# Attention output projection: VectorE adds each tile to the residual straight from PSUM, in place of a ScalarE copy and a GpSimd sum

## The chip, the core and the metric

The kernel runs on one core of a Trainium2 chip. The metric is the device time of one execution in microseconds (us), the median of several runs. A core has TensorE (PE in the profile: matmuls and transposes; PEld is its weight load), VectorE (DVE), ScalarE (ACT) and GpSimd (POOL), each with its own queue that it works off in order, and SyncE, which starts DMA transfers. Engines wait for each other by semaphores. Matmul results land in PSUM, which has eight banks of 128 partitions by 512 float32 values.

## The reference, cut to what matters

One pre-norm decoder layer on `x` of shape (4, 512, 512): attention, a small cross attention, and a mixture of experts. The change touches the end of the attention:

```python
q = (xn @ Wq.T).reshape(B, L, 32, 64)      # 32 query heads
k = (xn @ Wk.T).reshape(B, L, 8, 64)       # 8 key/value heads
v = (xn @ Wv.T).reshape(B, L, 8, 64)
q, k = rope(q), rope(k)
p = softmax(causal(q @ k.T) / 8)
out = (p @ v).reshape(B, L, 2048)
x = x + out @ Wo.T                         # the change is in this line
```

Every float32 matmul is made of products of a high and a low part (`_hi`, `_lo`): ACT writes the rounded high part, and DVE or POOL subtracts it from the source to get the low part.

## The kernel before, in words

Everything stays in SBUF during the attention: the residual `x_res`, the normalised input `xn_hi`, `xn_lo`, and the weights of one key/value group. The outer loop runs over the 8 groups (`GROUPS`), inside it over the 4 batches (b = 0 to 3), inside that over the 4 query heads of the group (h = 0 to 3). The work of one (b, h) is called a slot here; there are 16 in a group and 128 in all. In a slot the heads are software-pipelined. For slot c = 4b + h, PE issues, in this order:

- the last two transposes of the head two before (`pe_ptrans`, u = 2, line 218), which wait until DVE has made `pt_lo` from the bank that they overwrite;
- the scores of the next head (line 208);
- for h = 0, 1, 2 a projection of the next batch (line 185, 12 matmuls), for h = 3 only four small transposes of v (line 195);
- in slot h = 0 an output projection (t = 2, line 247);
- eight transposes of the previous head (u = 0 and 1, line 218), the first of which wait until DVE has made the `pt_lo` of the u = 2 transposes above;
- probabilities times v (line 235);
- in slots h = 1, 2 and 3 an output projection (t = 3, 0 and 1, line 247).

So there is one output projection of 128 tokens (`pe_wo`, six matmuls into the bank `WO_BANK`) in each slot, 128 in all. Before the change ACT copies the bank to SBUF (`act_wo`, line 372, `wo_out`, two buffers), and POOL adds the copy to the residual (`pool_woacc`, line 562). ACT, DVE and POOL have orders of their own, written out by hand. For DVE in a slot: `dve_masked` (line 434: four rows of the next head's scores plus mask, with a row maximum), `pt_lo` for u = 2, in even slots `o_lo` (line 422), in slots h = 0 and h = 2 the two `q_st` low parts (lines 459 and 460), in slot h = 2 of b = 1 the two low parts of the output weights (`w_lo`, line 422), for h < 3 the rotary multiply and shuffle (lines 452 and 453), a reciprocal (line 441), `pt_lo` for u = 0 and 1, and `dve_oadd` (line 487, `o_f`), which waits for ACT's `act_opart`. For POOL in a slot: for h = 1 `k_lo` (line 554), for h < 3 the rotary sum (lines 537 and 539), the normalisation of the probabilities (`pool_norm`, line 546, four pieces), the sum of the change (line 562), and in slots h = 1, 2, 3 of b = 2 the low part of one third of the next group's projection weights (`w1_lo`, line 469, also called `w_lo` in the rows).

The next output projection waits on `wo_out_done`, since there is one bank. The last group's last batch has no next batch to project, and its four output projections come at the very end, each in a bank of its own. After the attention a second block begins (cross attention and routing), and after it the experts, in which the change touches nothing.

Of the kernel before, what the change touches and what calls it, by code (L numbers as in the profile page):

```python
# [21 lines left out]
ALU = mybir.AluOpType  # L22
ACT = mybir.ActivationFunctionType
# [43 lines left out]
def wait(eng, sem, value):  # L67

    if isinstance(value, int) and value <= 0:
        return  # L70
    eng.wait_ge(sem, value)
# [27 lines left out]
def decoder_layer(nc, x, ctx, ctx_cols, mem_mask, wqkv, wo_rows, router_cols, router_b, gu_w, gu_b, down_w, down_b,  # L99
                  cos_t, sin_t, causal_t, ident_t, iota_t, out):  # L100
    stack = ExitStack()
    with stack:
# [24 lines left out]
        def sa(name, shape, dt=F32):  # L127
            return attn.enter_context(nc.sbuf_tensor(name, shape, dt))
# [14 lines left out]
        v_st = sa("v_st", [P, 2, QB, P], F32R)  # L143
        rot = sa("rot", [P, L])
        rope = sa("rope", [P, 2, L])
        wo_out = sa("wo_out", [P, 2, D])
        v_and_o = sa("v_and_o", [P, L])
        o_part, v_t = v_and_o[0:HD, :], v_and_o[HD:P, :]
        o_f = sa("o_f", [P, L])
# [12 lines left out]
            "w2_lo_done", "proj_done", "vt_done", "rope_in", "rot_sin", "rope_sum", "rope_hi", "k_lo_done", "q_lo_done",  # L162
            "v_tr", "v_hi_done", "v_lo_done", "scores_done", "masked_done", "exp_done",
            "recip_done", "pnorm_done", "ptrans_done", "pt_hi_done", "pt_lo_done", "pv_done", "opart_done",
            "oadd_done", "o_hi_done", "o_lo_done", "wo_done", "wo_out_done", "woacc_done")}

        def settled(eng):

# [196 lines left out]
            wait(act, s["wo_done"], 4 * m - 4)  # L365
            act_split(o_st[0][:, k, :], o_f[:, :], s["o_hi_done"])

        def act_wo(act, m, t, src=WO_BANK):

            act.wait_ge(s["wo_done"], 4 * m + t + 1)  # L370
            wait(act, s["woacc_done"], 4 * m + t - 1)
            nc.scalar.activation(wo_out[:, t % 2, :], src[:, :], ACT.Copy).then_inc(s["wo_out_done"], 1)  # L372

        def act_group(act, g, r):

            for c in range(HEADS + (isinstance(g, int) and g == GROUPS - 1)):
                b, h = divmod(c, G)
                n, m = HEADS * g + c, B * g + b
                front = c < HEADS
                begun = not (isinstance(g, int) and g == 0 and c == 0)  # L380
                more = not (isinstance(g, int) and g == GROUPS - 1 and c >= HEADS - 1)
                next_batch = not (isinstance(g, int) and g == GROUPS - 1 and b >= B - 1)
                d = c - 1
                db, dh = divmod(d, G)
                dn_, dm = HEADS * g + d, B * g + db
                d_here = not (isinstance(g, int) and g == 0 and d < 0)
                d_begun = not (isinstance(g, int) and g == 0 and d < 1)
                d_last = not (isinstance(g, int) and g == 0 and db < 1)
                d_before_last = not (isinstance(g, int) and g == 0 and db < 2)
                if d_begun:  # L390
                    act_pt(act, dn_ - 1, (d + 1) % 2, 2)
                if h == 0 and begun and front:
                    act_rope(act, m, 2, b % 2)
                if h in (1, 2) and next_batch:
                    act_rope(act, m + 1, h - 1, (b + 1) % 2)
                if more:
                    act_exp(act, n + 1, (r + c + 1) % 3)
                if h == 0 and next_batch:
                    act_vt(act, m + 1, 3 * m + 4)
                if d_here:  # L400
                    act_pt(act, dn_, d % 2, 0)
                    act_pt(act, dn_, d % 2, 1)
                if dh == 3 and d_last:
                    act_wo(act, dm - 1, 2)
                if h == 3 and next_batch:
                    act_v(act, m + 1, (b + 1) % 2)
                if d_begun:
                    act_opart(act, dn_ - 1)
                if dh in (1, 2) and d_last:
                    act_wo(act, dm - 1, dh - 1)  # L410
                if dh == 0 and d_before_last:
                    act_wo(act, dm - 2, 3)
                if d_begun and dh % 2 == 0:
                    act_o(act, dn_ - 1, dm if dh else dm - 1, (d // 2 - 1) % 4)
                if dh == 0 and db == 1:
                    act_w2(act, g)
                if (b, h) in W1_SLOTS and not (isinstance(g, int) and g == GROUPS - 1):
                    act_w1(act, g + 1, W1_SLOTS[b, h])
# [70 lines left out]
        def dve_o(dve, pair, k):  # L489
            dve.wait_ge(s["o_hi_done"], pair + 1)  # L490
            dve_lo(o_st[1][:, k, :], o_f[:, :], o_st[0][:, k, :], s["o_lo_done"])

        def dve_group(dve, g, r):

            for c in range(HEADS + (isinstance(g, int) and g == GROUPS - 1)):
                b, h = divmod(c, G)
                n, m = HEADS * g + c, B * g + b
                front = c < HEADS
                begun = not (isinstance(g, int) and g == 0 and c == 0)
                more = not (isinstance(g, int) and g == GROUPS - 1 and c >= HEADS - 1)  # L500
                next_batch = not (isinstance(g, int) and g == GROUPS - 1 and b >= B - 1)
                d = c - 1
                db, dh = divmod(d, G)
                dn_, dm = HEADS * g + d, B * g + db
                d_here = not (isinstance(g, int) and g == 0 and d < 0)
                d_begun = not (isinstance(g, int) and g == 0 and d < 1)
                d_last = not (isinstance(g, int) and g == 0 and db < 1)
                d_before_last = not (isinstance(g, int) and g == 0 and db < 2)
                if more:
                    dve_masked(dve, n + 1, (r + c + 1) % 3)  # L510
                if d_begun:
                    dve_pt(dve, dn_ - 1, (d + 1) % 2, 2)
                if d_begun and dh % 2 == 1 and not (isinstance(g, int) and g == 0 and d == 1):
                    dve_o(dve, HEADS // 2 * g + (d - 1) // 2 - 1, ((d - 1) // 2 - 1) % 4)
                if h == 0 and begun and front:
                    dve_q_lo(dve, m, 2, b % 2)
                if h == 2 and next_batch:
                    dve_q_lo(dve, m + 1, 1, (b + 1) % 2)
                if dh == 1 and db == 1:
                    dve_w2(dve, g)  # L520
                if h < 3 and next_batch:
                    dve_rope_in(dve, m + 1, h, (b + 1) % 2)
                if more:
                    dve_recip(dve, n + 1, (r + c + 1) % 3)
                if d_here:
                    dve_pt(dve, dn_, d % 2, 0)
                    dve_pt(dve, dn_, d % 2, 1)
                if h == 3 and next_batch:
                    dve_v(dve, m + 1, (b + 1) % 2)
                if d_begun:  # L530
                    dve_oadd(dve, dn_ - 1, (d - 1) % 2, HEADS // 2 * g + (d - 1) // 2)


        def pool_rope(pool, m, r, mb):
# [13 lines left out]
        def pool_k_lo(pool, m, mb):  # L548

            pool.wait_ge(s["rope_hi"], 6 * m + 2)  # L550
            wait(pool, s["pnorm_done"], 16 * m - 8)
            wait(pool, s["woacc_done"], 4 * m - 9)
            for half_ in range(2):
                nc.gpsimd.tensor_tensor(k_lo[half_ * HD:(half_ + 1) * HD, mb, :], rope[0:HD, mb, :], k_hi[0:HD, mb, :].bitcast(F32),
                                        ALU.subtract).then_inc(s["k_lo_done"], 1)
            pool.wait_ge(s["k_lo_done"], 2 * m + 2)

        def pool_woacc(pool, m, b, t):

            pool.wait_ge(s["wo_out_done"], 4 * m + t + 1)  # L560
            tile = x_res[:, b * QB + t, :]
            nc.gpsimd.tensor_tensor(tile, wo_out[:, t % 2, :], tile, ALU.add).then_inc(s["woacc_done"], 1)  # L562

        def pool_group(pool, g, r):

            for c in range(HEADS + (isinstance(g, int) and g == GROUPS - 1)):
# [16 lines left out]
                    pool_rope(pool, m + 1, h, (b + 1) % 2)  # L583
                if more:
                    pool_norm(pool, n + 1, (r + c + 1) % 3)
                if dh and d_last:
                    pool_woacc(pool, dm - 1, (db - 1) % B, dh - 1)
                if dh == 0 and d_before_last:
                    pool_woacc(pool, dm - 2, (db - 2) % B, 3)
                if (b, h) in W1_SLOTS and not (isinstance(g, int) and g == GROUPS - 1):  # L590
                    w1_lo(nc.gpsimd, pool, g + 1, W1_SLOTS[b, h])

# [12 lines left out]
        with nc.Block() as block:  # L605
# [51 lines left out]
            def _(act):  # L657
# [25 lines left out]
                act_pt(act, HEADS * GROUPS - 1, 1, 2)  # L683
                act_opart(act, HEADS * GROUPS - 1)
                act_o(act, HEADS * GROUPS - 1, B * GROUPS - 1, 3)
                act_wo(act, B * GROUPS - 2, 3)
                for t in range(QB):
                    act_wo(act, B * GROUPS - 1, t, (*S_BANK, PJ_BANK)[t])

            @block.vector  # L690
            def _(dve):
# [36 lines left out]
                dve_pt(dve, HEADS * GROUPS - 1, 1, 2)  # L728
                dve_oadd(dve, HEADS * GROUPS - 1, 1, HEADS * GROUPS // 2 - 1)
                dve_o(dve, HEADS * GROUPS // 2 - 1, 3)  # L730

            @block.gpsimd
            def _(pool):
# [17 lines left out]
                    for i in range(1, 4):  # L751
                        pool_group(pool, 3 * q + i, i % 3)
                pool_group(pool, GROUPS - 1, (GROUPS - 1) % 3)
                pool_woacc(pool, B * GROUPS - 2, B - 2, 3)
                for t in range(QB):
                    pool_woacc(pool, B * GROUPS - 1, B - 1, t)

        attn.close()

# [910 lines left out]
```

## Time and profile before

| | before |
|---|---|
| median of 3 runs | 1655.32 us (1653.87 to 1656.75) |
| the profiled execution | 1654.71 us, span 1653.0 us |
| PE, PEld busy | 1487.3 us (90%), 1305.1 us (79%) |
| DVE busy | 1329.5 us (80%) |
| ACT busy | 1113.7 us (67%) |
| POOL busy | 1049.0 us (63%) |
| attention (0 to 1066 us): the change's stage | 64% of the span |
| mean granted TensorE clock | 0.954 |

A busy PE isn't a PE at its peak: matmuls are pipelined, so their durations overlap in the rows. What matters is where PE stands idle, and for whom. A row of the timeline has the start, the duration, the engine, the line, the operation with what it writes and reads, and, in brackets, how long the engine stood idle before it and which instruction ended the wait.

### The profile page before, as it was taken

Reading aid. Unit: us, or ns where it says so; the run is one execution under the profiler, and the core shown is the slowest. Engines: PE = TensorE matmul, PEld = TensorE weight load, DVE = VectorE, ACT = ScalarE, POOL = GpSimd, SP = SyncE. Lnnn points to the kernel's source line nnn. Section 1 sums busy time; section 2 is a strip of 40 time slices with the busy share of each in tenths; the row PEclk is TensorE's granted clock in tenths of the full one; section 3 lists DMA queues with packets and bytes.
Section 4 is the critical chain, followed back from the end, with each engine's and each line's share of the span. In section 5 each row is a group of like instructions: output and inputs, shape, how many; then the busy total and the mean of one; then the engine's idle time right before and its main releaser. Section 6 shows DMA issues by size and latency. Waiting matters only on the chain. (4 is left out here: it accounts for less than half of the span.)

```text
span 1653.0 us, 31706 instructions
## 1 busy us (share of the span) xinstructions
PE 1487.3 (90%) x8951; PEld 1305.1 (79%) x8951; DVE 1329.5 (80%) x3470; ACT 1113.7 (67%) x2593; POOL 1049.0 (63%) x1161
## 2 busy tenths in 40 slices
PE   5799999999999999999999999698689999999994
PEld 4678888888888778878878877577479999999993
DVE  7688888888888888888888888388678998898892
ACT  3687887887887788788778878432156666666661
POOL 6668878878878878878878877556613223322321
PEclk9799999999999999999999999967589999999997
DMA  4000000000000000000000000112368878888775
GB/s 173 1 13 20 2 14 20 1 14 20 1 14 21 3 14 20 1 14 20 1 14 1 1 1 1 41 64 90 108 213 230 238 218 217 232 236 219 196 180 134
DMA packets 62033, 124.98 MB, mean 76 GB/s; under 512 B 20942, under 2 KB 21070, under 8 KB 61792
## 3 DMA queue, kind: packets, MB, share of 16 engines
q1 hardware_dynamic: 51408, 102.24, 19.5%
q0 software_dynamic: 10304, 20.59, 6.6%
q8 instruction: 77, 1.26, 0.3%
q14 instruction: 100, 0.82, 0.2%
q10 hardware_dynamic: 144, 0.07, 0.0%
HBM read 106.08 MB, written 24.71 MB: 79 GB/s over the span
## 5 line engine op out<-in xcount | busy, mean ns | idle before, releaser
L546 POOL TENSOR_SCALAR probs<-probs,row_inv 128x512 f32<-128x512 f32 (+3 forms) x512 | 303.6, 614 | 15.1 <-DVE row_inv L441 15.1
L313 ACT ACTIVATE probs<-probs,neg_max 128x512 f32<-128x512 f32 (+3 forms) x512 | 281.7, 552 | 28.5 <-DVE neg_max L434 25.6
L434 DVE CUSTOM_DVE_ANT_0 probs<-bank,causal 128x512 f32<-128x512 f32 (+3 forms) x512 | 220.5, 485 | 54.6 <-PE bank L208 53.7
L1246 POOL DMA_INDIRECT acc<-ctx_raw,idx x46 | 74.6, 1621 | 294.3 <-ACT ctx_raw L1399 280.0
L218 PE MATMUL bank<-ident,probs 128*128 128x128 f32 x1280 | 185.0, 275 | 60.1 <-DVE pt_lo L422 55.7
L422 DVE TENSOR_TENSOR pt_lo<-bank,pt_hi 128x512 fp32r<-128x512 f32 (+1 forms) x384 | 216.3, 591 | 26.2 <-ACT pt_hi L306 26.2
L218 PEld LDWEIGHTS bank<-ident,probs 128*128 128x128 f32 x1280 | 149.7, 141 | 96.8 <-DVE pt_lo L422 58.8
L537 POOL TENSOR_TENSOR rot<-rot,sin 128x512 f32<-128x512 f32 (+1 forms) x96 | 123.6, 1287 | 156.2 <-DVE rot L453 151.7
L1327 PE MATMUL bank<-xt_hi,gu_hi 128*128 128x256 f32 x736 | 208.1, 283 | 2.0 <-DVE xt_lo L422 1.5
L1327 PE MATMUL bank<-xt_hi,gu_lo 128*128 128x256 f32 x736 | 206.3, 280 | 0.0
L1327 PE MATMUL bank<-xt_lo,gu_hi 128*128 128x256 f32 x736 | 206.3, 280 | 0.0
L306 ACT ACTIVATE pt_hi<-bank 128x512 fp32r<-128x512 f32 (+1 forms) x384 | 184.9, 515 | 29.8 <-PE bank L218 26.7
L562 POOL TENSOR_TENSOR x_res<-wo_out,x_res 128x512 f32<-128x512 f32 x128 | 168.6, 1317 | 24.6 <-ACT wo_out L372 24.3
L208 PE MATMUL bank<-k_hi,q_st 128*128 128x256 f32 (+2 forms) x512 | 173.4, 349 | 2.7 <-DVE xn_lo L422 2.7
L235 PE MATMUL bank<-pt_hi,v_st 128*128 128x256 f32 (+2 forms) x512 | 170.5, 344 | 1.5 <-DVE pt_lo L422 1.5
L208 PE MATMUL bank<-k_lo,q_st 128*128 128x256 f32 (+2 forms) x512 | 157.4, 329 | 0.0
L235 PE MATMUL bank<-pt_lo,v_st 128*128 128x256 f32 (+2 forms) x512 | 155.0, 325 | 0.0
L185 PE MATMUL bank<-xn_hi,w_hi 128*128 128x512 f32 x384 | 152.8, 398 | 0.2 <-DVE rot L453 0.2
L185 PE MATMUL bank<-xn_lo,w_hi 128*128 128x512 f32 x384 | 151.5, 394 | 0.0
L185 PE MATMUL bank<-xn_hi,w_lo 128*128 128x512 f32 x384 | 151.1, 394 | 0.0
L1327 PEld LDWEIGHTS bank<-xt_hi,gu_hi 128*128 128x128 f32 x736 | 138.9, 189 | 6.0 <-issue 2.8
L1327 PEld LDWEIGHTS bank<-xt_lo,gu_hi 128*128 128x128 f32 x736 | 139.2, 189 | 3.0
(203 smaller groups left out, 4077.4 us busy)
## 6 DMA issues: line engine op xcount, KB each, us to landing
gu_raw<-in_gate_up SPq DMA_DIRECT2D x92, 512.0 KB, 4.2
dn_raw<-in_down SPq DMA_DIRECT2D x92, 256.0 KB, 3.7
w_raw<-in_wqkv SPq DMA_DIRECT2D x8, 768.0 KB, 4.5
w_raw<-in_wo_rows SPq DMA_DIRECT2D x8, 512.0 KB, 3.6
h_rows<-ln_h SPq DMA_DIRECT2D x16, 256.0 KB, 2.0
acc<-x_res SPq DMA_DIRECT2D x4, 1024.0 KB, 4.8
x_res<-in_x SPq DMA_DIRECT2D x3, 1024.0 KB, 11.3
ctx_raw<-in_ctx SPq DMA_DIRECT2D x2, 512.0 KB, 6.5
```

What stands on the lines that cost most here:

```text
L185: last = nc.tensor.matmul(PJ_BANK[:, :], w1[sp][:, c, r * P:(r + 1) * P], xn[mp][:, c, b * L:(b + 1) * L], start=first, stop=(c == DC - 1 ...
L208: last = nc.tensor.matmul(S_BANK[k][:, at:at + cols], q_st[:, h, i * P:(i + 1) * P], kk[:, kb, 0:cols], start=(a == 0), stop=(a == 1))
L218: last = nc.tensor.transpose(T_BANK[u % 2][:, k * P:(k + 1) * P], probs[:, hb, P_AT[i] + j * P:P_AT[i] + (j + 1) * P], ident[:, :])
L235: last = nc.tensor.matmul(dst, v_st[:, vb, j, :], rhs, start=(j == 0 and a == 0), stop=(j == QB - 1 and a == 1))
L306: nc.scalar.activation(dst, src, ACT.Copy).then_inc(sem_, 1)
L313: nc.scalar.activation(row, row, ACT.Exp, bias=neg_max[:, hb, i:i + 1], scale=-1.0, accum_out=row_sum[:, hb, i:i + 1]).then_inc(s["exp_don ...
L422: nc.vector.tensor_tensor(dst, src, hi.bitcast(F32), ALU.subtract).then_inc(sem_, 1)
L434: nc.vector.tensor_tensor_reduce(out=probs[:, hb, P_AT[i]:P_AT[i] + (i + 1) * P], in0=S_BANK[k][:, at:at + (i + 1) * P], in1=causal[:, (QB ...
L537: nc.gpsimd.tensor_tensor(rot[0:rows, :], rot[0:rows, :], sin[0:rows, :], ALU.mult).then_inc(s["rot_sin"], 1)
L546: nc.gpsimd.tensor_scalar(row, row, row_inv[:, hb, i:i + 1], 0.0, ALU.mult, ALU.add).then_inc(s["pnorm_done"], 1)
L562: nc.gpsimd.tensor_tensor(tile, wo_out[:, t % 2, :], tile, ALU.add).then_inc(s["woacc_done"], 1)
L1327: last = nc.tensor.matmul(GU_BANK[u % 3][:, side * TILE:(side + 1) * TILE], gu[sp_][:, ib, c, side, :], xts[mp][:, k, c, :], start=first, ...
```

## The change

DVE reads the output projection's bank and the residual tile, and writes the sum to the residual. ACT's 128 copies, POOL's 128 sums, the buffer `wo_out` and the semaphore `woacc_done` go. On DVE the sum has the place in the slot that ACT's copy had on ACT: in slot h = 0 between `pt_lo` and `dve_oadd` (t = 2), in the others behind `dve_oadd` (t = 3, 0, 1), and the last five at the end of the attention.

```diff
-        wo_out = sa("wo_out", [P, 2, D])
...
-        def act_wo(act, m, t, src=WO_BANK):
-
-            act.wait_ge(s["wo_done"], 4 * m + t + 1)
-            wait(act, s["woacc_done"], 4 * m + t - 1)
-            nc.scalar.activation(wo_out[:, t % 2, :], src[:, :], ACT.Copy).then_inc(s["wo_out_done"], 1)
...
+        def dve_woacc(dve, m, b, t, src=WO_BANK):
+
+            dve.wait_ge(s["wo_done"], 4 * m + t + 1)
+            tile = x_res[:, b * QB + t, :]
+            nc.vector.tensor_tensor(tile, src[:, :], tile, ALU.add).then_inc(s["wo_out_done"], 1)
...
+                if dh == 3 and d_last:
+                    dve_woacc(dve, dm - 1, (db - 1) % B, 2)
                 if h == 3 and next_batch:
                     dve_v(dve, m + 1, (b + 1) % 2)
                 if d_begun:
                     dve_oadd(dve, dn_ - 1, (d - 1) % 2, HEADS // 2 * g + (d - 1) // 2)
+                if dh in (1, 2) and d_last:
+                    dve_woacc(dve, dm - 1, (db - 1) % B, dh - 1)
+                if dh == 0 and d_before_last:
+                    dve_woacc(dve, dm - 2, (db - 2) % B, 3)
...
-            wait(pool, s["woacc_done"], 4 * m - 9)
...
-        def pool_woacc(pool, m, b, t):
-
-            pool.wait_ge(s["wo_out_done"], 4 * m + t + 1)
-            tile = x_res[:, b * QB + t, :]
-            nc.gpsimd.tensor_tensor(tile, wo_out[:, t % 2, :], tile, ALU.add).then_inc(s["woacc_done"], 1)
...
+                dve_woacc(dve, B * GROUPS - 2, B - 2, 3)
+                for t in range(QB):
+                    dve_woacc(dve, B * GROUPS - 1, B - 1, t, (*S_BANK, PJ_BANK)[t])
```

(`d` is the slot before `c`, so dh = 3 is in slot h = 0, dh = 0 in h = 1, dh = 1 in h = 2, dh = 2 in h = 3.)

## Rows read from the trace of the kernel before

**Rows 1.** Busy time of a stretch: length, PE, PEld, DVE, ACT, POOL, clock, DMA.
```profile
120.00:1000.00 880.00, 823.57 (x4705) 710.85 (x4704) 726.80 (x1918) 706.64 (x1771) 724.75 (x806) 1.00 0.03 10
```
**Rows 2.** Waits of PE from 120 to 1000 us: total, times, longest.
```profile
PE bank L218 <- DVE pt_lo L422: 42.0, 46, 1.6
PE bank L247 <- DVE w_lo L422: 11.2, 7, 1.8
```
**Rows 3.** Groups by shape, 120 to 1000 us: busy, mean ns | idle before, releaser.
```profile
L562 POOL TENSOR_TENSOR x_res<-wo_out,x_res 128x512 f32<-128x512 f32 x112 | 148.0, 1321 | 8.8 <-ACT wo_out L372 8.8
L372 ACT ACTIVATE wo_out<-bank 128x512 f32<-128x512 f32 x112 | 67.2, 600 | 64.3 <-PE bank L247 64.1
L452 DVE TENSOR_TENSOR rope<-bank,cos 128x512 f32<-128x512 f32 x56 | 38.6, 690 | 30.9 <-PE bank L185 30.3
```
**Rows 4.** Timeline of PE in one group: the four kinds of gaps.
```profile
730.92 0.49 PE L247 MATMUL bank<-w_hi,o_hi 128*128 128x512 f32 x1 [1.59 <-DVE w_lo L422]
...
766.14 1.09 PE L218 MATMUL bank<-ident,probs 128*128 128x128 f32 x8 [1.06 <-DVE pt_lo L422]
...
779.27 0.44 PE L218 MATMUL bank<-ident,probs 128*128 128x128 f32 x2 [1.59 <-DVE pt_lo L422]
...
795.43 0.44 PE L218 MATMUL bank<-ident,probs 128*128 128x128 f32 x2 [0.33 <-DVE pt_lo L422]
```
**Rows 5.** Timeline of DVE, end of b = 2, h = 1 to b = 3, h = 0.
```profile
754.66 0.68 DVE L487 TENSOR_TENSOR o_f<-bank,v_and_o 64x512 f32<-64x512 f32 x1 [0.21 <-ACT v_and_o L306]
756.22 0.69 DVE L434 CUSTOM_DVE_ANT_0 probs<-bank,causal 128x512 f32<-128x512 f32 x1 [0.87 <-PE bank L208]
...
758.20 0.69 DVE L422 TENSOR_TENSOR o_lo<-o_f,o_hi 128x512 fp32r<-128x512 f32 x1
759.11 0.78 DVE L459 TENSOR_TENSOR q_st<-rope,q_st 64x512 fp32r<-64x512 f32 x1 [0.21 <-ACT q_st L306]
759.90 0.87 DVE L460 TENSOR_TENSOR q_st<-rope,q_st 64x512 fp32r<-64x512 f32 x1
760.80 0.69 DVE L452 TENSOR_TENSOR rope<-bank,cos 128x512 f32<-128x512 f32 x1
...
761.42 0.74 DVE L453 STREAM_SHUFFLE rot<-bank 128x512 f32<-128x512 f32 x1
...
763.31 0.68 DVE L487 TENSOR_TENSOR o_f<-bank,v_and_o 64x512 f32<-64x512 f32 x1
764.02 0.69 DVE L434 CUSTOM_DVE_ANT_0 probs<-bank,causal 128x512 f32<-128x512 f32 x1
...
772.72 3.08 DVE L422 TENSOR_TENSOR o_lo<-o_f,o_hi 128x512 fp32r<-128x512 f32 x1
```
**Rows 6.** Timeline of POOL: b = 1, h = 2; b = 2, h = 2; b = 3, h = 0.
```profile
728.54 1.70 POOL L562 TENSOR_TENSOR x_res<-wo_out,x_res 128x512 f32<-128x512 f32 x1
...
757.66 3.36 POOL L546 TENSOR_SCALAR probs<-probs,row_inv 128x512 f32<-128x512 f32 x4
...
762.24 1.30 POOL L469 TENSOR_TENSOR w_lo<-w_raw,w_hi 128x512 fp32r<-128x512 f32 x1
...
772.70 1.31 POOL L562 TENSOR_TENSOR x_res<-wo_out,x_res 128x512 f32<-128x512 f32 x1
773.95 1.31 POOL L469 TENSOR_TENSOR w_lo<-w_raw,w_hi 128x512 fp32r<-128x512 f32 x1
```
**Rows 7.** The tile `w_lo` on DVE, 728 to 731.2 us: least/median/most ns, starts.
```profile
L422 DVE TENSOR_TENSOR w_lo<-w_raw,w_hi x2: 749/1252/1754, 728.4 to 729.0; 128x512 fp32r<-128x512 f32 x2
```
**Rows 8.** Timeline of ACT: the changed copies, and a high part in b = 3, h = 0.
```profile
763.31 0.60 ACT L372 ACTIVATE wo_out<-bank 128x512 f32<-128x512 f32 x1 [0.32 <-PE bank L247]
...
770.96 0.62 ACT L306 ACTIVATE w_hi<-w_raw 128x512 fp32r<-128x512 f32 x1
...
1063.75 0.60 ACT L372 ACTIVATE wo_out<-bank 128x512 f32<-128x512 f32 x1 [0.76 <-PE bank L247]
```
**Rows 9.** Timeline of POOL at the attention's end: the last four sums.
```profile
1060.33 5.36 POOL L562 TENSOR_TENSOR x_res<-wo_out,x_res 128x512 f32<-128x512 f32 x4 [1.16 <-ACT wo_out L372]
```

More of the change, by code:

```diff
@@ L164, in decoder_layer @@
             "recip_done", "pnorm_done", "ptrans_done", "pt_hi_done", "pt_lo_done", "pv_done", "opart_done",
-            "oadd_done", "o_hi_done", "o_lo_done", "wo_done", "wo_out_done", "woacc_done")}
+            "oadd_done", "o_hi_done", "o_lo_done", "wo_done", "wo_out_done")}
         def settled(eng):
@@ L402, in act_group @@
                     act_pt(act, dn_, d % 2, 1)
-                if dh == 3 and d_last:
-                    act_wo(act, dm - 1, 2)
                 if h == 3 and next_batch:
@@ L408, in act_group @@
                     act_opart(act, dn_ - 1)
[L409 to L412, printed above, removed]
                 if d_begun and dh % 2 == 0:
@@ L585, in pool_group @@
                     pool_norm(pool, n + 1, (r + c + 1) % 3)
[L586 to L589, printed above, removed]
                 if (b, h) in W1_SLOTS and not (isinstance(g, int) and g == GROUPS - 1):
@@ L685, in _ @@
                 act_o(act, HEADS * GROUPS - 1, B * GROUPS - 1, 3)
-                act_wo(act, B * GROUPS - 2, 3)
-                for t in range(QB):
-                    act_wo(act, B * GROUPS - 1, t, (*S_BANK, PJ_BANK)[t])
             @block.vector
@@ L753, in _ @@
                 pool_group(pool, GROUPS - 1, (GROUPS - 1) % 3)
-                pool_woacc(pool, B * GROUPS - 2, B - 2, 3)
-                for t in range(QB):
-                    pool_woacc(pool, B * GROUPS - 1, B - 1, t)
         attn.close()
```

## The prediction

> **What bounds the kernel now.** First the busy time of a long stretch. In the attention's steady part PE is busy 823.6 of 880 us (94%), DVE 726.8 (83%), POOL 724.8 (82%), ACT 706.6 (80%), the TensorE clock is at its full 2.4 GHz (1.00) and DMA is at 0.03 [rows 1]. So PE bounds this stage, and the most that any change can win here is the rest, some 56 us, unless it takes work off PE, which this one doesn't. Next, for whom PE waits: 42.0 us for DVE's `pt_lo`, 11.2 us for DVE's `w_lo`, for ACT's copy and POOL's sum not at all [rows 2]. The change takes work from two engines that PE doesn't wait for and puts it on the one that it does wait for. By sums of busy time it is bad. Whether it is depends on where in the order the gaps lie, and on what makes DVE late there.
>
> The timeline of PE shows a pattern that repeats in each of the 8 groups (880 us hold seven, so one has about 125 us) [rows 4]. (a) In slot h = 3 of all four batches 1.06 us before the eight transposes, since with no projection in this slot PE gets there before DVE has done four rows of `dve_masked` and one `pt_lo`. (b) In b = 1, slot h = 2, 1.59 us for `w_lo`. (c) In b = 3, slot h = 0's end, 1.59 us for `pt_lo`. (d) In b = 3, slot h = 2's end, 0.33 us.
>
> Behind (b) and (c) stands a collision. `o_lo` with both inputs in SBUF takes 0.69 us, but 3.08 us when it starts at 772.72, beside POOL's sum of the change (772.70 to 774.01) and POOL's `w_lo` behind it (to 775.26): it ends 0.54 us after the second of them [rows 5, 6]. The same in b = 1: DVE's second `w_lo` starts at 729.0 and takes 1754 ns, to 730.75, half a microsecond after POOL's sum ended at 730.24 [rows 6, 7]. In the other direction, the four pieces of POOL's normalisation take 3.36 us while DVE works on `o_lo` and the two `q_st`, which themselves take 0.78 and 0.87 us [rows 5, 6]. So while POOL reads two SBUF tensors, a DVE operation with two SBUF inputs stands still.
>
> **The change part by part.** *Added:* 128 DVE sums of a PSUM and an SBUF tile, 128x512. That shape is there: the rotary multiply, mean 690 ns [rows 3]; the next instruction starts 0.62 us after it [rows 5]. It isn't stretched by POOL, as its PSUM input leaves one SBUF input only. I take 0.62 us a piece (0.69 as upper bound): 79 us on DVE in all. *Removed:* 128 copies of 600 ns on ACT and 128 sums of 1321 ns on POOL [rows 3], with their waits (ACT stands idle 64.1 us before the copies, so it also stops blocking `act_o` and `act_pt` behind them) and the `woacc_done` waits. No DMA is touched, PE's work is the same.
>
> *Where the 0.62 us lies,* by slot. At the boundary h = 1 to 2 DVE stands idle 0.87 us for the scores between `o_f` and `dve_masked`: `o_f` ends at 755.34, PE goes from the output projection straight to the scores, so the bank is ready about when DVE's idle time begins, and `dve_masked` starts at 756.22 [rows 5]. The sum fits, with 0.2 us to spare; the boundary h = 3 to 0 is like it. In slot h = 0 it stands before `oadd`, and what it delays has the twelve matmuls of the next slot's projection to catch up. Both cost 0. At the boundary h = 2 to 3 there is no such room: `o_f` ends at 763.99, `dve_masked` starts at 764.02 [rows 5], and this is what gap (a) waits for. Here the full 0.62 us counts, in each batch, unless DVE arrives earlier.
>
> *What makes DVE earlier in slot h = 2.* POOL without its sum begins `k_lo` and the rotary sums 1.3 us earlier, so ACT's `q_st` is no longer late (0.21 us of DVE's idle time [rows 5]) and the normalisation is over before the two `q_st` (0.09 + 0.18 us back, to 0.69 each). That is 0.48 us. `o_f` then starts at 762.83, the next instruction 0.62 later at 763.45, when the bank is ready (ACT's copy began at 763.31 [rows 8]), and `dve_masked` at 764.07 against 764.02. Per group then:
> - b = 0: no gain, no loss (0 to -0.15 us).
> - b = 1: in addition DVE's two `w_lo` meet no sum of POOL: 0.749 + 1.754 us [rows 7] become 1.4, 1.1 us won; 1.1 + 0.48 - 0.62 = +0.9 us. Gap (b) goes; part of what it gave comes back as a deeper gap (a).
> - b = 2: POOL's `w_lo` for the next group, at 762.24 before, has no sum ahead of it any more and follows the normalisation (which ended at 761.0, and now 1.3 us earlier for the sum that is gone and 1.3 for the stretch, at about 758.4) straight into DVE's `o_lo` and `q_st` (758.20 to 760.77) [rows 5, 6]. DVE loses there what it lost to the sum in b = 1, some 1.1 us, which takes the 0.48 back and leaves it 0.6 late; with 0.62 for the sum, -1.2 us.
> - b = 3: the normalisation no longer waits behind a sum, POOL's `w_lo` starts when ACT has made the high part (at 771.58, about 0.5 earlier without the copy [rows 8]) and ends at about 772.4, before `o_lo` is issued at 772.72 [rows 5, 6]. `o_lo` ends 2.4 us earlier; gap (c) is only 1.59 deep, so +1.59. If they still meet, 1.3. Gap (d), where `q_st` came late for the same reason, goes too: +0.33.
>
> Sum: 0 + 0.9 - 1.2 + 1.9 = 1.6 us a group. The next group's weights are made in seven of the eight: 7 x 1.6 = 11.2. In the last group b = 1 gives 0.9, b = 3 has no projections and its DVE chain is bare; I take -0.3 (0 to -0.6). End of the attention: ACT's last copy starts at 1063.75 [rows 8], POOL, at 1.3 us a sum, is done at 1065.69 [rows 9]; a DVE sum would be done at 1063.75 + 0.69 = 1064.44: 1.25 us won, and the next stage, which waits for all engines, follows. In all 11.2 + 0.9 - 0.3 + 1.25 = 13 us. Against the profiled execution, 1654.7 us (span 1653.0), which is 0.6 under the median 1655.3, I get 1641.7, say 1642 us.
>
> The weighing of a rule. DVE has the highest share after PE and is the only engine for which PE waits [rows 1, 2]. The Trainium skill, page "Perfetto Trace Analysis", section "Optimizing Scalar/DVE Operations", says that if DVE is saturated, moving work from it to Scalar or GPSIMD may make sense; that speaks against this change. The same section adds that moving work between GPSIMD and DVE may not help as they share an SBUF port. By the first sentence the time would be that of the second rival below, by the second that of my sum or near no change. By the rows DVE isn't saturated: 726.8 us and 112 new sums of 0.69 make 804 of 880 us, 91%.
>
> **The rivals.**
> 1. *More relief than I allow:* the collision in b = 2 doesn't happen, since ACT's high part or the port's order lets POOL's `w_lo` pass behind `q_st`. Then b = 2 costs nothing: 7 x 1.2 = 8.4 us more, 1633 to 1634 us. For it: DVE's `o_lo` took a plain 0.69 us amid the normalisation. Against: where POOL's `w_lo` met a DVE operation with two SBUF inputs, it took DVE's time. Chance 0.18.
> 2. *DVE becomes the bound in slot h = 2 to 3, and the relief doesn't come:* POOL isn't early enough, or collides elsewhere (its `k_lo` and rotary sums are movable too). Then each of 32 batches pays 0.62 us: +19.8, less 1.25 at the end: about 1673 us. It decides where the relief in slot h = 2 falls under 0.62 us and no collision is removed. For it: rows 2, and only 0.03 us of room. Against: both large gaps follow from the very sum that goes. Chance 0.18.
> 3. *It evens out:* one of the reliefs fails (b = 3's 1.9, or 0.9 in b = 1 together with more loss in b = 2): 7 x 1.9 = 13 us less, so 1652 to 1658. Chance 0.14.
>
> My forecast has 0.50; its own range is 1636 to 1651, from the bounds above (7 x 0.3 for (c), 7 x 3 x 0.07 for the 0.69, 0.3 in the last group, and 0.6 us a group either way for how DVE and POOL meet in b = 2). The range for 8 times in 10 takes in rivals 1 and 3 and part of rival 2: 1631 to 1662. A measurement of this kernel tells 0.2%, 3.3 us, from no change. Faster by more: forecast and rival 1, 0.68; within: rival 3, 0.13; slower: 0.19.
>
> **What the profile of the changed kernel would show.** DVE has 128 groups more of 0.69 us, busy 1329 + 88 less the stretches that vanish (7 x (2.4 + 1.1) = 25 us); POOL's busy time falls by 169 us and some stretches and ACT's by 77. Right: no `o_lo` over 1 us in b = 3, slot h = 0; `w_lo` on DVE about 0.7 us each; the PE gaps of 1.59 us gone, those in h = 3 about 1.1 us in b = 0 and 3, and 2 us or more in b = 2 together with stretched `q_st` or `o_lo`; the next stage begins some 13 us earlier. Wrong would be: a masked row that waits in slots h = 1 or h = 0 behind the new sum, a new sum of well over 0.69 us, PE waiting for `wo_out_done`, or POOL's `k_lo`, now earlier, falling on DVE's SBUF operations.

## The result and the profile after

Four runs of the changed kernel have a median of 1642.06 us (1635.15 to 1643.71), beside 1655.05 us for the kernel before. The ratio is 0.9919, with a 95% interval of 0.9905 to 0.9932: 0.8% faster, 13.0 us. Forecast was 1642. The profiled execution took 1642.2 us, span 1640.4.

First line of the page's busy times, then PE's waits from 120 to 990 us, where the earlier view went to 1000 us [rows 2]:

```profile
PE 1484.6 (91%) x8951; PEld 1306.0 (80%) x8951; DVE 1382.3 (84%) x3598; ACT 1057.5 (64%) x2465; POOL 849.1 (52%) x1033
```
```profile
PE bank L217 <- DVE pt_lo L409: 37.8, 39, 2.6
PE bank L217 <- POOL probs L545: 5.9, 4, 1.7
```

POOL is 200 us less busy: 169 us are the sums that went, and most of the rest is the normalisation, which takes 264.2 us in place of 303.6. The 5.9 us for POOL are gap (a) in the first and the last group, and the wait of 2.6 us stands at the loop's end (below). DVE has 128 sums more, but is only 53 us busier. The wait for DVE's `w_lo` (11.2 us) is gone. The tiles `o_lo` and `w_lo` in the attention say where most of the other 35 us of DVE went (columns: count, least/median/most ns):

```profile
L409 DVE TENSOR_TENSOR o_lo<-o_f,o_hi x62: 680/683/824, 112.7 to 1043.7; 128x512 fp32r<-128x512 f32 x62
...
L409 DVE TENSOR_TENSOR w_lo<-w_raw,w_hi x15: 683/684/694, 99.7 to 968.1; 128x512 fp32r<-128x512 f32 x15
```

These are 23 of the 35 us: the 64 `o_lo` take 15.1 us less in all (62.0 to 46.9) and the 16 `w_lo` 8.0 us less (18.3 to 10.3); the two `q_st` give 2 more. The rest is mostly overlap of rows, since a sum's row lasts 0.67 to 0.69 us and the next instruction starts 0.60 us after it where nothing holds it up. No `o_lo` of 3.08 us, no `w_lo` of 1754 ns any more [rows 5, 7]. PE's timeline over one group, with b = 1, b = 2, b = 3 and the next b = 0, to be read beside [rows 4]:

```profile
724.68 0.44 PE L217 MATMUL bank<-ident,probs 128*128 128x128 f32 x2 [0.15 <-DVE pt_lo L409]
...
728.45 1.09 PE L217 MATMUL bank<-ident,probs 128*128 128x128 f32 x8 [1.54 <-DVE pt_lo L409]
...
755.88 0.44 PE L217 MATMUL bank<-ident,probs 128*128 128x128 f32 x2 [0.28 <-DVE pt_lo L409]
...
759.64 0.55 PE L217 MATMUL bank<-ident,probs 128*128 128x128 f32 x3 [1.53 <-DVE pt_lo L409]
```
```profile
789.85 1.09 PE L217 MATMUL bank<-ident,probs 128*128 128x128 f32 x8 [1.15 <-DVE pt_lo L409]
...
820.06 1.09 PE L217 MATMUL bank<-ident,probs 128*128 128x128 f32 x8 [1.15 <-DVE pt_lo L409]
```

Both gaps of 1.59 us (b, c) and the one of 0.33 (d) are gone. Gap (a) is 1.15 in b = 0 and 3, but 1.54 in b = 1 and 1.53 in b = 2, which has 0.28 more ahead of it. Why b = 2 is late is in DVE's and POOL's timelines:

```profile
747.08 0.68 DVE L474 TENSOR_TENSOR o_f<-bank,v_and_o 64x512 f32<-64x512 f32 x1 [0.21 <-ACT v_and_o L305]
747.84 0.69 DVE L484 TENSOR_TENSOR x_res<-bank,x_res 128x512 f32<-128x512 f32 x1
748.63 0.69 DVE L421 CUSTOM_DVE_ANT_0 probs<-bank,causal 128x512 f32<-128x512 f32 x1
...
750.62 0.80 DVE L409 TENSOR_TENSOR o_lo<-o_f,o_hi 128x512 fp32r<-128x512 f32 x1
751.44 1.66 DVE L446 TENSOR_TENSOR q_st<-rope,q_st 64x512 fp32r<-64x512 f32 x1
753.12 0.69 DVE L447 TENSOR_TENSOR q_st<-rope,q_st 64x512 fp32r<-64x512 f32 x1
...
756.34 0.67 DVE L474 TENSOR_TENSOR o_f<-bank,v_and_o 64x512 f32<-64x512 f32 x1
756.94 0.67 DVE L484 TENSOR_TENSOR x_res<-bank,x_res 128x512 f32<-128x512 f32 x1
757.54 0.67 DVE L421 CUSTOM_DVE_ANT_0 probs<-bank,causal 128x512 f32<-128x512 f32 x1
```
```profile
750.83 1.73 POOL L456 TENSOR_TENSOR w_lo<-w_raw,w_hi 128x512 fp32r<-128x512 f32 x1
...
759.91 1.28 POOL L456 TENSOR_TENSOR w_lo<-w_raw,w_hi 128x512 fp32r<-128x512 f32 x1
...
764.66 1.30 POOL L456 TENSOR_TENSOR w_lo<-w_raw,w_hi 128x512 fp32r<-128x512 f32 x1 [1.44 <-ACT w_hi L305]
```

The sum at the boundary h = 1 to 2 (747.84) lies wholly in what was idle time; the one at h = 2 to 3 (756.94) pushes the masked rows by 0.60 us. POOL's `w_lo` at 750.83, which stood behind the `q_st` at 762.24 before [rows 6], now meets the first `q_st`, which takes 1.66 in place of 0.69 us, and is itself held up (1.73 in place of 1.30 us). The 128 new sums read one tile from PSUM and one from SBUF, and none of them is stretched, though the one at 747.84, for example, stands beside POOL's rotary sum of two SBUF tiles (747.55 to 748.84):

```profile
L484 DVE TENSOR_TENSOR x_res<-bank,x_res x128: 669/691/693, 103.4 to 1050.2; 128x512 f32<-128x512 f32 x128
```

The third of POOL's `w_lo`, at 764.66, waits for ACT's high part and is clear of `o_lo`, whose 3.08 us it had helped to make.

The attention's end in DVE's timeline: the last sum ends at 1050.93 and the next block starts at 1051.30.

```profile
1050.24 0.69 DVE L484 TENSOR_TENSOR x_res<-bank,x_res 128x512 f32<-128x512 f32 x1 [0.67 <-PE bank L246]
1051.30 0.07 DVE L1501 MEMSET count<- 128x9 f32 x1 [0.37 <-PEq L593]
```

PE's first transpose of the next stage starts at 1057.28, before at 1072.09: 14.8 us earlier. The stages behind took 2.2 us longer in this execution. Over the twelve kernels below they took 579 to 585 us in the profiled execution, though nothing is changed there, so a single span says little under 3 us; the period of a group, which scatters far less, says more. I take it from PE's timeline, from an instruction to the same one a group later: 125.2 us before, 123.0 after (759.64 to 882.66).

### The profile page after: what moved, and what is told of

Read it like the earlier page. It is cut to its first block and busy times, and to the rows that moved or that the text cites. A ratio compares the mean times of both kernels' runs of the same rounds, so it can differ in the third digit from the quotient of the medians.

```text
span 1640.4 us, 31332 instructions
## 1 busy us (share of the span) xinstructions
PE 1484.6 (91%) x8951; PEld 1306.0 (80%) x8951; DVE 1382.3 (84%) x3598; ACT 1057.5 (64%) x2465; POOL 849.1 (52%) x1033
## 5 line engine op out<-in xcount | busy, mean ns | idle before, releaser
L545 POOL TENSOR_SCALAR probs<-probs,row_inv 128x512 f32<-128x512 f32 (+3 forms) x512 | 264.2, 534 | 42.8 <-DVE row_inv L428 42.8
L1312 PEld LDWEIGHTS bank<-xt_hi,gu_lo 128*128 128x128 f32 x736 | 138.9, 189 | 0.0
## 6 DMA issues: line engine op xcount, KB each, us to landing
x_res<-in_x SPq DMA_DIRECT2D x3, 1024.0 KB, 11.2
```

The source lines that it names most:

```text
L545: nc.gpsimd.tensor_scalar(row, row, row_inv[:, hb, i:i + 1], 0.0, ALU.mult, ALU.add).then_inc(s["pnorm_done"], 1)
L1312: last = nc.tensor.matmul(GU_BANK[u % 3][:, side * TILE:(side + 1) * TILE], gu[sp_][:, ib, c, side, :], xts[mp][:, k, c, :], start=first, ...
```

## The experiments

Each was run beside the kernel before on the same chip (median 1654.2 to 1654.8 us there); the ratios are to it. The changed kernel wasn't run again beside them, so a difference from its 1642.06 us is sure only to some 4 us. The periods of a group are from the profiled executions, in the middle of the attention and away from the loop's end.

**GpSimd's work put back.**

```diff
+        def pool_idle_sum(pool, m, t):
+            pool.wait_ge(s["wo_out_done"], 4 * m + t + 1)
+            wait(pool, s["woacc_done"], 4 * m + t - 1)
+            nc.gpsimd.tensor_tensor(wd[:, t % 2, :], cos[:, :], sin[:, :], ALU.add).then_inc(s["woacc_done"], 1)
...
+                if dh and d_last:
+                    pool_idle_sum(pool, dm - 1, dh - 1)
+                if dh == 0 and d_before_last:
+                    pool_idle_sum(pool, dm - 2, 3)
```

> The changed kernel, and GpSimd does a sum of the same size as the old one (cosine plus sine table into a buffer nobody reads) at the old places and with the old waits, except for the last five at the end of the attention. The residual is computed as in the changed kernel. Theory (the gain is GpSimd's absence from the SBUF that VectorE reads): all reliefs are undone and VectorE's 0.62 us in slots h = 2 to 3 stay, so 1654.7 + 32 x 0.62 - 1.25 = about 1673 us, with o_lo of about 3 us and w_lo of 1.7 us back. Rival (the gain is ScalarE's copy that is gone, or the shorter way of the result): 1642 to 1645 us.

1669.4 us, ratio 1.010 (1.0081 to 1.0118): 27 us slower than the changed kernel, 15 slower than before, near the theory's 1673 and far from its rival. A group takes 126.5 us. `o_lo` and DVE's `w_lo` are long again:

```profile
L410 DVE TENSOR_TENSOR o_lo<-o_f,o_hi x61: 679/683/2604, 115.6 to 1063.7; 128x512 fp32r<-128x512 f32 x61
```
```profile
L410 DVE TENSOR_TENSOR w_lo<-w_raw,w_hi x16: 685/752/1755, 100.3 to 993.7; 128x512 fp32r<-128x512 f32 x16
```

So without GpSimd's relief the change would have made the kernel slower, as the prediction's second rival said. By this difference DVE's sums cost 15 us or more while GpSimd does its own, and without these they cost 9.4 (below): the relief also made them cheaper.

**The same with work on GpSimd that reads no SBUF.**

```diff
-            wait(pool, s["woacc_done"], 4 * m + t - 1)
-            nc.gpsimd.tensor_tensor(wd[:, t % 2, :], cos[:, :], sin[:, :], ALU.add).then_inc(s["woacc_done"], 1)
+            wait(pool, s["woacc_done"], 4 * m + t)
+            settled(pool)
+            nc.gpsimd.memset(wd[:, :, :], 0.0).then_inc(s["woacc_done"], 1)
```

> As the kernel with GpSimd's idle sum, but in its place a memset of 128x1024 into the buffer that nobody reads, about as long, which reads no SBUF. Theory (two things made VectorE late: the sum's reading collided with VectorE's SBUF operations, and GpSimd's own queue ran late behind it): only the second stays, 1650 to 1660 us, and w_lo of VectorE takes 0.7 us twice. Rival (GpSimd's late queue is all): 1667 to 1671 us as with the idle sum. Rival (the collision with the sum is all): 1642 to 1645 us.

1650.3 us, ratio 0.9974 (0.9961 to 0.9987). It lies at the lower end of the theory's range and outside both rivals. The lines are against the kernel with the idle sum; each memset also waits for the one before it, since all write one buffer. The memsets take 954 ns, three quarters of a sum, and DVE's `w_lo` is short:

```profile
L410 DVE TENSOR_TENSOR w_lo<-w_raw,w_hi x14: 683/690/694, 224.7 to 973.4; 128x512 fp32r<-128x512 f32 x14
```

Of the 27 us, 19 go with the sum's reads (its 0.35 us more of length included, which no run separates) and 8 stay with a longer queue. Both of the theory's parts are there, the collision is the larger. What stays shows in two ways. In the group from 700 to 825 us gap (a) is 1.5 us in all four batches, where the changed kernel has 1.15 in two. And POOL's normalisation, late behind the memset, stands beside DVE's operations of two SBUF inputs: at 753.76 it takes 2.93 us in place of 2.07, `o_lo` beside it 0.91, and the median `o_lo` 823 ns in place of 683. So part of the "queue" looks like a second, milder meeting in SBUF, which no run separates.

**ScalarE's work put back.**

```diff
+        def act_idle_copy(act, m, t):
+            act.wait_ge(s["wo_done"], 4 * m + t + 1)
+            nc.scalar.activation(wd[:, t % 2, :], cos[:, :], ACT.Copy)
...
+                if dh == 3 and d_last:
+                    act_idle_copy(act, dm - 1, 2)
...
+                if dh in (1, 2) and d_last:
+                    act_idle_copy(act, dm - 1, dh - 1)
+                if dh == 0 and d_before_last:
+                    act_idle_copy(act, dm - 2, 3)
```

> The changed kernel, and ScalarE does a copy of the same size as the old one (cosine table into a buffer nobody reads) at the old places, except for the last five. Theory: ScalarE has room everywhere; only the high part of the weights in b = 3, slot h = 0 comes 0.5 us later, so that GpSimd's w_lo may brush o_lo: 0 to +4 us, 1642 to 1646 us. Rival (ScalarE's relief brought the gain): 1650 us or more.

1647.6 us, ratio 0.9954 (0.9937 to 0.9970): 5.5 us slower than the changed kernel, 1.5 over the theory's end and below the rival's. A group takes 123.4 us, 0.4 more, so some 3 us are steady; a gap of up to 0.3 us for `w_lo` is back in b = 1, and b = 3 is 0.2 us longer too. ScalarE's relief has a share, which the prediction put at nothing: 3 us by the groups, 5.5 by the medians, whose intervals don't touch (the changed kernel's ends at 0.9932). The old copy read a bank and this one reads SBUF, so it stands for the time on ScalarE and not for the rest.

**VectorE's cost taken away.**

```diff
-            nc.vector.tensor_tensor(tile, src[:, :], tile, ALU.add).then_inc(s["wo_out_done"], 1)
+            nc.vector.tensor_tensor(tile[:, 0:1], src[:, 0:1], tile[:, 0:1], ALU.add).then_inc(s["wo_out_done"], 1)
```

> The changed kernel with VectorE's sum over one column of the 512 (the other 511 columns of the projection are left out of the residual). It shows the changed kernel free of VectorE's cost. Theory: only the boundary h = 2 to 3 counts; per group the gaps fall by 0.1 + 0.5 + 0.5 + 0.1 us, and a little at the ends: -9 to -12 us, 1630 to 1633 us. Rival (VectorE is the bound all over the attention): 128 x 0.55 us less, about 1572 us.

1632.6 us, ratio 0.9866 (0.9847 to 0.9886). DVE's sums cost 9.4 us in all, where 128 of them are 532 ns shorter (152 in place of 684), 68 us of engine time. PE feels a seventh of it.

**The collision in b = 2 taken away.**

```diff
-                if (b, h) in W1_SLOTS and not (isinstance(g, int) and g == GROUPS - 1):
+                if b == 2 and h >= 2 and not (isinstance(g, int) and g == GROUPS - 1):
+                    if h == 2:
+                        w1_lo(nc.gpsimd, pool, g + 1, W1_SLOTS[2, 1])
                     w1_lo(nc.gpsimd, pool, g + 1, W1_SLOTS[b, h])
```

> The changed kernel; GpSimd makes the low part of the first third of the next group's weights in b = 2 one slot later (in slot h = 2, before that of the second third), away from VectorE's o_lo and q_st of that slot. Theory (the collision costs b = 2 its relief): gaps of b = 2 fall from 0.3 + 1.5 us to about 1.2 us, 7 x 0.65 = 4.5 us less, 1637 to 1638 us, and q_st no longer takes 1.7 us there. Rival (b = 2 is late for the sum alone): no change, 1641.5 to 1642.5 us.

1639.1 us, ratio 0.9910 (0.9888 to 0.9933). By the times alone it can't be told from the changed kernel. The trace is clear: a group takes 122.2 us, 0.9 less, the first `q_st` takes 684 to 689 ns throughout, and in b = 2 the gaps 0.28 and 1.53 have become one of 1.19:

```profile
L446 DVE TENSOR_TENSOR q_st<-rope,q_st x56: 684/685/689, 129.6 to 974.6; 64x512 fp32r<-64x512 f32 x56
```
```profile
661.22 1.09 PE L217 MATMUL bank<-ident,probs 128*128 128x128 f32 x8 [1.19 <-DVE pt_lo L409]
```

**The sum t = 0 moved into idle time.**

```diff
                 if d_begun:
                     dve_pt(dve, dn_ - 1, (d + 1) % 2, 2)
+                if dh == 2 and d_last:
+                    dve_woacc(dve, dm - 1, (db - 1) % B, 0)
...
-                if dh in (1, 2) and d_last:
-                    dve_woacc(dve, dm - 1, (db - 1) % B, dh - 1)
+                if dh == 2 and d_last:
+                    dve_woacc(dve, dm - 1, (db - 1) % B, 1)
```

> The changed kernel with the sum t = 0 moved from the end of slot h = 2 into slot h = 3, behind the four masked rows and pt_lo, where VectorE stands idle some 0.9 us for ScalarE's exponentials. Nothing is left out. Theory (the sum costs only at the boundary h = 2 to 3): most of what the one-column sum gave comes back, 7 x 1.3 = 9 us, 1632 to 1635 us. Rival (VectorE's total load binds): no change, 1641 to 1643 us.

1633.2 us, ratio 0.9880 (0.9853 to 0.9906), as fast as with one column, and a group takes 121.9 us here and 122.0 there: within the scatter, the whole cost of DVE's sums was that one boundary.

**The loop's end.**

```diff
-                with pe.Fori(0, (GROUPS - 2) // 3) as q:
-                    for i in range(1, 4):
-                        pe_group(pe, 3 * q + i, i % 3)
+                if True:
+                    for i in range(1, GROUPS - 1):
+                        pe_group(pe, i, i % 3)
...
```

> The changed kernel with the loop over groups 1 to 6 (two rounds of three groups) written out on PE, ACT, DVE and POOL. The profile shows the stretch over the loop's end 7 us longer than other groups (PE idle 2.6 us for pt_lo, DVE 3.5 us and ACT 5.0 us of issue), in the kernel before 2 us longer. Theory (the loop's end gives back some 5 us of the gain): 1635 to 1637.5 us, and no gap over 2 us there. Rival (chance of one execution): 1641 to 1643 us.

> The kernel before with the same loop written out. Theory: the loop's end costs it 2 us: 1652 to 1653.5 us. Rival (as much as in the changed kernel, and the profiled execution was a lucky one): 1648 to 1650 us.

The reason for these two is the place where the loop starts its second round, in the changed kernel's timelines of PE and DVE:

```profile
540.97 0.43 PE L217 MATMUL bank<-ident,probs 128*128 128x128 f32 x2 [0.46 <-issue]
...
552.05 0.44 PE L217 MATMUL bank<-ident,probs 128*128 128x128 f32 x2 [2.60 <-DVE pt_lo L409]
```
```profile
544.76 0.69 DVE L421 CUSTOM_DVE_ANT_0 probs<-bank,causal 128x512 f32<-128x512 f32 x1 [3.53 <-issue]
```

Written out, the changed kernel takes 1640.2 us, ratio 0.9924 (0.9898 to 0.9949), and the kernel before 1650.4, ratio 0.9977 (0.9966 to 0.9988). The first lies between its theory and its rival, the second just above its rival. In both profiles the long batch is gone: 35.8 and 32.0 us became 30.2. But in time the changed kernel gains 2 us where 5 were expected, and the kernel before 4 where 2 were. That the loop's end gives back more of the change's gain than it cost before is so in the profiled executions and not in the medians; it stays open. Part of the 35.8 us isn't the loop: the granted clock fell there for a few microseconds (last section). Without such a fall the batch took 34.5 us with the one column and 34.1 with the sum t = 0 moved, 4 us more than its like, against 2 in the kernel before.

**Three moves together.** The two moves above, and in slot h = 3 `pt_lo` ahead of the masked rows:

```diff
+                if d_begun and h == 3:
+                    dve_pt(dve, dn_ - 1, (d + 1) % 2, 2)
                 if more:
                     dve_masked(dve, n + 1, (r + c + 1) % 3)
-                if d_begun:
+                if d_begun and h != 3:
                     dve_pt(dve, dn_ - 1, (d + 1) % 2, 2)
```

> The changed kernel with three moves: GpSimd's first third of w_lo one slot later, the sum t = 0 in slot h = 3, and in slot h = 3 VectorE's pt_lo (u = 2) ahead of the four masked rows, so that PE's eight transposes there don't wait for these (gap a, 1.05 us in each of 32 batches). Nothing is left out. Theory (gap a is a chain scores, masked rows, pt_lo, not a lack of VectorE time): 1642 - 4.5 - 8 - 30 = about 1600 us, 1597 to 1608 us. Rival (VectorE, at 89% busy, is the bound and gives nothing more): 1628 to 1636 us.

1616.6 us, ratio 0.9776 (0.9754 to 0.9798). Better than the rival, short of the theory by 8 us or more. The shortfall lies in the third move: by themselves the first two gave 3 and 9 us, near the 4.5 and 8 of the sum, so that, if gains add, the third gave some 13 of its 30. PE's waits from 120 to 980 us, 12.5 us where the changed kernel had 37.8 from 120 to 990:

```profile
PE bank L217 <- DVE pt_lo L409: 12.5, 35, 1.1
```

In this stretch PE is busy 843.62 of 860 us (98%) and DVE 781.70 (91%). What is left are mostly gaps of 0.2 to 0.6 us. A group takes 119.4 us. With the loop written out:

> The three moves, and the loop over groups 1 to 6 written out. Theory: the batch over the loop's end, 34.0 us in the profile against 29.5 us elsewhere, falls to 29.5: 4.5 us less, 1611 to 1613 us. Rival (no effect beyond the scatter of the executions): 1615 to 1618 us.

1609.9 us, ratio 0.9726 (0.9708 to 0.9744), just below the theory's range, and the batch over the loop's end takes 29.5 us: the fastest, 45 us under the kernel before and 32 under the changed one, with the whole computation.

**That order alone,** on the kernel before and on the changed one:

> The kernel before, and in slot h = 3 VectorE's pt_lo (u = 2) stands ahead of the four masked rows; ScalarE's copy and GpSimd's sum stay. Theory (gap a is an order, in both kernels; the collisions of gaps b to d are not touched by it): about 3 us a group of the 4.2 in gap a, 1654 - 24 = 1630 us, 1625 to 1635 us. Rival (the order only pays with the change, since VectorE is held up by GpSimd): 1645 us or more.

> The changed kernel with pt_lo (u = 2) ahead of the masked rows in slot h = 3 and nothing else moved. Theory (with that order PE doesn't wait for the masked rows, so the 0.62 us before them and the collision in b = 2 cost little more): 1617 to 1624 us, near the three moves. Rival (the moves' gains are of separate waits and add up): 1616.5 + 9 + 3, about 1629 us.

1644.5 us, ratio 0.9937 (0.9920 to 0.9955), and 1634.9, ratio 0.9889 (0.9863 to 0.9914). Both miss the theory: 10 and 7 us in place of 24 and at least 18. The first meets its rival's 1645 us within the scatter, the second is slower than its theory and its rival. In the kernel before, PE now reaches the collisions earlier and waits there; these gaps were 1.59 us in both places [rows 4]:

```profile
647.33 0.44 PE L218 MATMUL bank<-ident,probs 128*128 128x128 f32 x2 [2.15 <-DVE pt_lo L422]
```
```profile
723.01 0.49 PE L247 MATMUL bank<-w_hi,o_hi 128*128 128x512 f32 x1 [1.79 <-DVE w_lo L422]
```

Its groups take 123.4 us where they are shortest, 1.8 less than before, and up to 125.7; the granted clock fell six times in this attention, one of them right behind the second of these waits.

In the changed kernel the sum t = 0 still stands ahead of `pt_lo`. The single moves on the changed kernel give 3, 9 and 7 us, together 19, and all three at once 25.5. That fits a reading in which gap (a) was slack where DVE caught up each batch, so that its removal pays only as far as DVE isn't late for other reasons; but an excess of 6.5 us over a sum of three differences is hardly beyond their scatter, and the kernel with the first two moves alone, which would tell, wasn't run.

## Why the prediction was right, point by point

*DVE's price.* 0.62 us to the next instruction, 0.69 alone: measured 0.60 (756.94 to 757.54) and a mean of 684 ns, never over 693.

*Where it lies.* Hidden at h = 1 to 2, h = 3 to 0 and in h = 0, counted at h = 2 to 3: borne out by one column (1632.6) and by moving that one sum (1633.2), which agree. DVE went from 80% to 84% of the span, and in the attention from 83% to 89% (770.05 of 870 us), and moving 128 operations onto this busiest of the elementwise engines paid. The Trainium skill, page "Perfetto Trace Analysis", section "Optimizing Scalar/DVE Operations", says that moving work off DVE may make sense where DVE is saturated. This case doesn't contradict it, since at 89% DVE wasn't, but a high share alone would have pointed the wrong way. The same section of the Trainium skill says that moving work between GPSIMD and DVE might not help, because they share an SBUF read port. Here it did help, by 0.8%. The reason given agrees with the runs, in reverse: GpSimd's reads stood in DVE's way (27 us with the idle sum, 8 with the memset), and a DVE sum with one input in PSUM was never stretched.

*The relief.* Collisions of GpSimd's sum with DVE's SBUF operations: shown by the idle sum (+27 us) against the memset (+8). Which of GpSimd's operations made which of DVE's late is in the rows: `o_lo` and `w_lo` are long with the sums and short without, and `q_st` is long in b = 2 until GpSimd's `w_lo` is moved.

*Terms of the sum.* Per group, in one execution of each kernel. The length of a batch is taken from the start of its predecessor's eight transposes behind gap (a) to its own (703.57, 736.03, 766.14, 798.72, 828.83 us before; 697.06, 728.45, 759.64, 789.85, 820.06 after):

| batch | predicted | gaps before | gaps after | won by gaps | length before, after | won by length |
|---|---|---|---|---|---|---|
| b = 0 | 0 | 1.05 | 1.15 | -0.1 | 30.11, 30.21 | -0.1 |
| b = 1 | +0.9 | 1.59 + 0.17 + 1.05 | 0.15 + 1.54 | +1.1 | 32.46, 31.39 | +1.1 |
| b = 2 | -1.2 | 1.06 | 0.28 + 1.53 | -0.75 | 30.11, 31.19 | -1.1 |
| b = 3 | +1.9 | 1.59 + 0.33 + 1.05 | 1.15 | +1.8 | 32.58, 30.21 | +2.4 |

The lengths sum to 2.3 against 1.6, and the group's period fell by 2.2. They are the measure, because a wait costs PE more than the idle time that its row shows. Gap (c) is 1.59 us deep, but from the matmul before it to the transposes are 1.87 us, where the changed kernel, without the wait, needs 0.12:

```profile
777.40 0.28 PE L235 MATMUL bank<-pt_lo,v_st 128*128 128x256 f32 x1
779.27 0.44 PE L218 MATMUL bank<-ident,probs 128*128 128x128 f32 x2 [1.59 <-DVE pt_lo L422]
```
```profile
770.90 0.28 PE L234 MATMUL bank<-pt_lo,v_st 128*128 128x256 f32 x1
771.02 0.38 PE L217 MATMUL bank<-ident,probs 128*128 128x128 f32 x2
```

So the mis-sized term is b = 3: I took the depth of gaps (c) and (d), 1.9 us, for what they cost, and it was 2.4. b = 2 came as worked out: the collision cost 0.97 us on `q_st` and 0.11 on `o_lo`, 1.1 in all, and the batch grew by 1.1 us. A term put at nothing is ScalarE's relief for its own sake, 0.4 us a group by the copy put back, 0.2 of it each in b = 1 and b = 3.

Seven groups give 15.4 us, 4 more than my 11.2. In the profiled execution they came back behind the loop's end, which I hadn't foreseen: a group there took up to 7 us more than its like, where it took 2 more before. Of the 7 us some 3 are two short falls of the granted clock (last section) and 4 are the loop's end. The end of the attention, 1.25 us: the last sum starts with the projection done and ends 0.69 us later, and from that projection's first matmul to the next stage there are 12.8 us in place of 14.1, as worked out. So the mechanism was right, but that its sum, 13 us, is the measured number is luck: terms too small by 4 us, 5 us lost behind the loop's end, 2 us won by another clock at the start and 2 us lost in the stages behind happen to cancel.

*Secondary numbers.* DVE's busy time was to rise by about 63 us and rose by 53: the long operations gave back the 25 us foretold, and the rest is the overlap of rows. ACT's was to fall by 77 and fell by 56; in part that is overlap too, as the instruction behind a copy started 0.1 us before the copy's end (13 us over the 128 copies). POOL's fell by 200, of which I had named 169 "and some stretches".

## What to carry to other kernels

Cost an operation by where it stands in its engine's order and not by the engine's busy share: 68 us of VectorE time cost 9, all at one boundary of four. Take what a wait costs from the distance between the instructions on either side of it and not from the idle time alone. Before a move between VectorE and GpSimd, look for VectorE operations with two SBUF inputs whose longest duration is far above their median, and ask which GpSimd operation stands beside them; then ask where the other GpSimd work will fall once it runs earlier. Expect little from removing one wait where the engine that causes it is late elsewhere too: the same move brought 10 us of an expected 24 and 7 of at least 18.

## What was unexpected of the hardware

The granted clock early in the kernel differs between executions without a change in the work of that stretch. From 40 to 80 us, where nothing of the change runs yet, it was 0.87 in the changed kernel and 0.79 in the one before (the number after POOL's busy time):

```profile
40.00:80.00 40.00, 27.92 (x145) 23.89 (x145) 28.88 (x79) 24.51 (x65) 26.92 (x34) 0.87 0.00 1
```
```profile
40.00:80.00 40.00, 28.60 (x132) 24.21 (x133) 26.54 (x76) 23.32 (x62) 25.13 (x32) 0.79 0.01 1
```

The batch there took 30.4 and 32.8 us, so some 2 us of the 14.8 by which the next stage starts earlier are this. The fourteen profiled executions fall into two kinds: seven with 0.87, whose batch took 30.2 to 30.5 us, and seven with 0.79, at 32.1 to 32.8. Changed kernels are among both (with the idle sum, the idle copy, the one column and the three moves with the loop written out it was 0.79), so the change alone doesn't set it; what does stays open. In these 40 us, PE was busy for only part of the time (27.9 and 28.6 of 40 us).

The clock also falls for a few microseconds in the middle of the attention, between none and six times in the fourteen profiled executions: twice in the changed kernel's, once in the other's. In these stretches of 10 us around two of them part of the time was at the lower of its two levels, 1.2 GHz, and the mean was 0.83:

```profile
600.00:610.00 10.00, 8.35 (x42) 7.34 (x43) 7.09 (x19) 5.48 (x15) 6.17 (x10) 0.83 0.11 43
```
```profile
980.00:990.00 10.00, 7.26 (x36) 6.12 (x37) 7.78 (x20) 5.69 (x16) 7.89 (x10) 0.83 0.00 0
```

A batch with such a fall takes 1.4 to 1.8 us more than its like: 32.8 in place of 31.2 us for the first of these, 33.8 in place of 32.4 for the second. PE stood in a wait before several of them (1.53 us at 603.88, 1.78 at 981.70, and 2.60 at 552.05 ahead of the fall at the loop's end), but waits as long as the first stand in the other groups with no fall behind them. So a single execution hides differences of 2 to 5 us, which the period of a group without a fall shows to 0.1 us.
